# One decoder block on one core: the planner's table of instruction times booked at the distance to the next instruction

## The chip, the core and the metric

The kernel runs on one core of a Trainium2 chip, in 32-bit floats throughout. The metric is device time in microseconds, from one launch. TensorE (PE) multiplies and transposes, VectorE (DVE), ScalarE (ACT) and GpSimd (POOL) work elementwise, SyncE (SP) issues most of the DMAs. Each engine works through a program of its own in order and waits on semaphores.

## What is computed

The reference is a decoder block over 8 rows of 256 tokens with width 256: two Mamba layers, a cross attention, and a mixture of 8 experts with the two best for each token, each followed by a residual and a layer norm. Cut to what matters:

```
for layer in range(2):                                   # Mamba, on x
    u, z = split(x @ in_w.T);  u = silu(causal_conv4(u))
    dt, B, C = split(u @ xp_w.T);  dt = softplus(dt @ dtw.T + dtb)
    h[t] = h[t-1] * exp(dt[t] * A) + (dt[t] * u[t]) * B[t]      # 512 channels x 64 states
    y[t] = sum_over_states(h[t] * C[t]) + u[t] * D_skip
    x = (y * silu(z)) @ out_w.T
x = norm(x0 + x);  x = norm(x + attention(x, ctx));
x = norm(x + sum_k w_k * (relu(x @ w1[e_k] + b1[e_k]) @ w2[e_k] + b2[e_k]))
```

## The kernel before

**Jobs and scans.** One Mamba layer of one row is a job; there are 16, in the order row 0 layer 0, row 1 layer 0, row 0 layer 1, and so on, so that the last job (15) is layer 1 of row 7. A job has 64 states, and each state is one step of the loop: 1024 steps in all, numbered i. In a step ScalarE makes the decay `dA` (L1152, four instructions), TensorE fills the PSUM tile `psX` (`fill_x`: either two transposes that spread B, L1461, after which VectorE multiplies, L1174; or, in a "turned" step, eight transposes of `xs`, L1474, or matmuls with `diag_b`, L1472, after which it need not), VectorE runs the scan over 4 x 256 elements (L1184), GpSimd multiplies with C (L954), and two steps later TensorE adds the product up by eight transposes into `psY` (L1490, `sum_states`). When a job's last state is summed, VectorE multiplies with the gate (L1199). `psX`, `dA`, `h` and `hC` have two or three buffers.

**Work beside the scans.** All other work is cut into tasks: the projections and the convolution of the next job (`tasks_pre`), the output of the last (`tasks_post`), the attention and routing of a finished row (`tasks_row`), and the experts (`tasks_experts`). The rows are routed in four groups of two. Each group gives 15 tiles of 128 slots (tiles 0 to 59; 45 to 59 belong to rows 6 and 7). A tile is gathered by a DMA, transposed (L1693), multiplied with the expert's first weights (8 tasks `hid`, L1437 with `xgT`, in quarters of 256 KB that arrive as `w_up`), goes through ScalarE (`relu`, L1104), is multiplied with the second weights (8 tasks `out`, L1516, `w_down`), copied (`y_copy`, L1111, into the one buffer `yg`) and stored to `y_slots` (L757). When all tiles of a group are stored, the rows are fetched (L916), blended (L1396), normed (`bn3`, `norm3`) and written out (`stored`, L839).

**What sets the order.** The class `Schedule` walks through the 1024 steps before anything is emitted. It keeps a clock for each engine, books each loop instruction and each task with a constant in ns, and puts into the list `beside[i]` those tasks that by its clocks still fit beside step i. The constants decide nothing at run time; they decide which task stands in which step in every engine's program, SP's list of DMAs included. Where the chains for rows and experts are empty, `keep_busy` fills a quarter of TensorE's free time with transposes that nobody reads (L1715). A step that has VectorE tasks is cut into two half scans with the tasks between (`splits`). What does not fit beside the loop stands behind it, in the list `tail`, ordered by `run_off`; there the weights may also use the `dA` and `h` buffers, so that nine quarters are in flight rather than three. The weights of a tile can be loaded only when the group's list of tiles exists (`list`, read by SP at L697).

## Time and profile before

| | us |
|---|---|
| median of 3 runs | 3357.46 (3356.96 to 3365.76) |
| span of the profiled execution | 3358.1 |
| VectorE busy | 3051.3 |
| TensorE busy | 2753.5 |
| ScalarE busy | 2744.4 |
| GpSimd busy | 2659.8 |

For the profiled execution only its span is given, 0.6 us above the median of the three runs. Busy time is the union of recorded lengths; an instruction's record can overlap the next one's, so the recorded length is more than the distance from one start to the next. A matmul of 32-bit operands shows as two records in the trace, a transpose as one.

### The profile page before, as it was taken

The page shows a single profiled execution, that of the slowest core. Times are in us where ns is not written, and L with a number is a line of the kernel's source. Part 1 is how long each engine was busy: PE and PEld are TensorE (multiplying, and loading weights), DVE is VectorE, ACT ScalarE, POOL GpSimd, SP SyncE. Part 2 cuts the span into 40 slices and gives each one's busy share as a digit, 9 for nine tenths or more (in the row PEclk, how much of TensorE's full clock was granted, in tenths as well). Part 3 has the DMA queues.
Part 4 walks back from the last instruction along what each step waited for, and adds up shares of the span by engine and source line. Part 5 has one row for each costly group of instructions (what it writes and reads, how often), then busy time and mean ns, then how long its engine had stood idle before and what let it go on. Part 6 is the DMA issues. An engine that isn't in the chain of part 4 may idle for free.

```text
span 3358.1 us, 55337 instructions
## 1 busy us (share of the span) xinstructions
PE 2753.5 (82%) x19829; PEld 2428.3 (72%) x19829; DVE 3051.3 (91%) x2211; ACT 2744.4 (82%) x6424; POOL 2659.8 (79%) x1289
## 2 busy tenths in 40 slices
PE   6888888887878877888888888878888777888877
PEld 5777777777767767677776777767777666777666
DVE  6999999999999999999999999999999999999510
ACT  7889898898878897897989888898898869888422
POOL 5989898898989788887888788787887878877311
PEclk8999999999999999999999998999999979999988
DMA  3341111111111113223331333313322122443476
GB/s 100 98 145 58 45 51 55 45 55 45 49 60 45 44 47 114 95 77 110 103 116 64 111 119 117 127 64 129 98 102 93 44 88 83 143 132 122 134 263 214
DMA packets 151750, 319.39 MB, mean 95 GB/s; under 512 B 28570, under 2 KB 44963, under 8 KB 151092
## 3 DMA queue, kind: packets, MB, share of 16 engines
q1 hardware_dynamic: 147522, 305.08, 27.5%
q0 software_dynamic: 3072, 8.39, 0.7%
q8 instruction: 158, 2.59, 0.3%
q10 hardware_dynamic: 882, 2.38, 0.2%
q14 instruction: 116, 0.95, 0.1%
HBM read 285.90 MB, written 29.88 MB: 94 GB/s over the span
## 4 chain that ended last, share of the span: by engine, by line
issue 27%; DVE 26%; POOL 19%; ACT 14%; PE 12%; DMA 2%; SPq 1%; POOLq 0%; DVEq 0%; ACTq 0%
POOL hC L954 17%; DVE h L1184 13%; DVE psX L1174 9%; ACT dA L1152 7%; PE psG L1437 3%; PE psY L1490 3%; ACT xs L1123 3%; PE psX L1516 2%; PE psX L1474 1%; PE psX L1472 1%; PE psX L1437 1%; PE psG L1516 1%; ACT gT L1003 1%; DVE gT L1199 1%; ACT scratch L1000 0%
## 5 line engine op out<-in xcount | busy, mean ns | idle before, releaser
L954 POOL TENSOR_TENSOR hC<-h,cb 128x1024 f32<-128x1024 f32 x1024 | 2406.2, 2371 | 496.2 <-DVE h L1184 487.4
L1184 DVE TENSOR_TENSOR_SCAN h<-dA,psX 128x1024 f32<-128x1024 f32 (+1 forms) x1115 | 2306.0, 2102 | 73.2 <-PE psX L1474 30.1
L1152 ACT ACTIVATE dA<-dt,negA 128x255 f32<-128x255 f32 x4096 | 1717.8, 503 | 107.0 <-DVE h L1184 104.9
L1490 PE MATMUL psY<-ident,hC 128*128 128x128 f32 x8192 | 1113.4, 281 | 54.1 <-DVE gT L1199 38.1
L1490 PEld LDWEIGHTS psY<-ident,hC 128*128 128x128 f32 x8192 | 968.1, 145 | 68.8 <-DVE gT L1199 41.7
L1174 DVE TENSOR_TENSOR psX<-dtu,psX 128x1024 f32<-128x1024 f32 x513 | 619.6, 1208 | 10.3 <-PE psX L1461 10.0
L1474 PE MATMUL psX<-ident,xs 128*128 128x128 f32 x3280 | 458.0, 285 | 146.5 <-ACT xs L1123 75.4
L1123 ACT ACTIVATE xs<-dtuT,bT 128x512 f32<-128x512 f32 x820 | 546.1, 719 | 11.9 <-PE psX L1474 11.4
L1474 PEld LDWEIGHTS psX<-ident,xs 128*128 128x128 f32 x3280 | 381.9, 146 | 218.2 <-ACT xs L1123 136.4
L1461 PE MATMUL psX<-ident,bT 128*128 128x128 f32 x1026 | 214.5, 292 | 181.8 <-DVE h L1184 179.8
L1461 PEld LDWEIGHTS psX<-ident,bT 128*128 128x128 f32 x1026 | 116.2, 139 | 283.3 <-DVE h L1184 263.8
L1472 PE MATMUL psX<-diag_b,dtuT 128*128 128x128 f32 x1616 | 212.8, 287 | 60.4 <-DVE h L1184 32.8
L1472 PEld LDWEIGHTS psX<-diag_b,dtuT 128*128 128x128 f32 x1616 | 196.6, 199 | 80.8 <-issue 41.4
L1437 PE MATMUL psG<-xgT,w_up 128*128 128x128 f32 x1456 | 204.2, 284 | 15.2 <-DMA w_up<-in_w_exp 9.1
L1437 PEld LDWEIGHTS psG<-xgT,w_up 128*128 128x128 f32 x1456 | 188.7, 199 | 25.5 <-DMA w_up<-in_w_exp 10.7
L1516 PE MATMUL psG<-w_down,hid 128*128 128x256 f32 x700 | 188.9, 392 | 7.7 <-ACT hid L1104 5.7
L1104 ACT ACTIVATE hid<-psG,b_tile 128x128 f32<-128x128 f32 x408 | 115.3, 366 | 60.7 <-PE psG L1437 60.5
L1516 PEld LDWEIGHTS psG<-w_down,hid 128*128 128x128 f32 x700 | 124.6, 196 | 27.7 <-ACT hid L1104 9.7
L1396 DVE SCALAR_TENSOR_TENSOR acc<-got,slot_weight,acc 128x256 f32<-128x256 f32 x28 | 14.7, 543 | 137.2 <-DMA got<-y_slots,slot_of 127.7
L916 POOL DMA_INDIRECT got<-y_slots,slot_of x28 | 29.1, 1039 | 127.5 <-DMA y_slots<-yg 117.6
L1437 PE MATMUL psG<-xin,w_in 128*128 128x256 f32 x256 | 70.0, 405 | 9.9 <-DMA conv_w<-in_conv 6.1
L1121 ACT ACTIVATE diag_b<-ident,bT 128x128 f32<-128x128 f32 x202 | 69.4, 394 | 4.0 <-PE psX L1472 4.0
(216 smaller groups left out, 2109.3 us busy)
## 6 DMA issues: line engine op xcount, KB each, us to landing
cb<-c_dram SPq DMA_DIRECT2D x256, 512.0 KB
w_up<-in_w_exp SPq DMA_DIRECT2D x196, 256.0 KB
w_down<-in_w_exp SPq DMA_DIRECT2D x196, 256.0 KB
dA<-in_w_exp SPq DMA_DIRECT2D x44, 256.0 KB, 5.5
h<-in_w_exp SPq DMA_DIRECT2D x44, 256.0 KB, 5.4
x_slots<-got SPq DMA_DIRECT2D x16, 512.0 KB, 5.7
xg<-x_slots SPq DMA_DIRECT2D x60, 128.0 KB
y_slots<-yg SPq DMA_DIRECT2D x60, 128.0 KB
```

The costliest lines, as they stand in the source:

```text
L954: eng.tensor_tensor(hC[i % NHC][:, :, :], h[i % NH][:, :, :], cw.to_broadcast([P, KI, L]), ALU.mult).then_inc(times_c, 1)
L1104: made = eng.activation(hid[part][:, i, :], bank[k][:, i * P:(i + 1) * P], ACT.Relu, bias=b1_tile[n % 2][:, c:c + 1])
L1123: made = eng.activation(xs[:, tc, :], dtuT[n % 2][:, tc, :], ACT.Identity, scale=bT[n % 2][:, tc, s:s + 1])
L1152: made = eng.activation(dA[j % NA][:, c, 1:L], dt[n % 2][:, c, 1:L], ACT.Exp, scale=negA[:, JOBS[n][0], c, s:s + 1])
L1174: eng.tensor_tensor(x[:, :, :], dtu[n % 2][:, :, :], x[:, KI - 1:KI, :].to_broadcast([P, KI, L]), ALU.mult).then_inc(times_b, 1)
L1184: made = eng.tensor_tensor_scan(h[i % NH][:, part, :].rearrange("p c t -> p (c t)"), dA[i % NA][:, part, :].rearrange("p c t -> p (c t)"), ...
L1437: made = eng.matmul(dst, lhs, rhs, start=begin and i == 0, stop=end and i == len(terms) - 1)
L1461: made = eng.transpose(psX[i % 2][:, KI - 1, tc * P:(tc + 1) * P], bT[n % 2][:, tc, s:s + 1].to_broadcast([P, P]), ident[:, :])
L1472: made = eng.matmul(to, dtuT[i // S % 2][:, tc, c * P:(c + 1) * P], diag_b[:, tc, :], start=True, stop=True)
L1474: made = eng.transpose(to, xs[:, tc, c * P:(c + 1) * P], ident[:, :])
L1490: made = eng.matmul(psY[:, tc, c * P:(c + 1) * P], hC[i % NHC][:, c, tc * P:(tc + 1) * P], ident[:, :], start=s == 0 and c == 0, stop=s == ...
L1516: made = eng.matmul(bank[k][:, 0:D], hid[half][:, i, :], w_down[slot][:, i % 2, :], start=half == i == 0, stop=half == 1 and i == 3, skip_ ...
```

## The change

The constants are replaced by smaller ones: `MM` (one `hid` or `out` task, half of most others) 520 to 450 ns, `TURN` 130 to 112, `EVICT` 620 to 500, `HALF_EVICT` 470 to 360, a `relu` 4 x 340 to 4 x 260, `SUM` 1060 to 900, `SPREAD` 280 to 250, `OUTER` 1060 to 920, a fill by `diag_b` 2 x 1060 to 1830, `SCALE` 1340 to 1230, the decay 1700 to 1600, the product with C 2380 to 2330, `SCAN` 2220 to 2200. Two are raised: `PRODUCT` 1210 to 1240, and `SPLIT`, the price of cutting a scan in two, 60 to 190. No function that emits instructions is touched.

```diff
-MM, TURN, EVICT, HALF_EVICT = 520, 130, 620, 470
+MM, TURN, EVICT, HALF_EVICT = 450, 112, 500, 360
...
-SUM, SPREAD, OUTER, SCALE, PRODUCT, SCAN, SPLIT = 1060, 280, 1060, 1340, 1210, 2220, 60
+SUM, SPREAD, OUTER, MULTIPLY, SCALE, DECAY, TIMES_C, PRODUCT, SCAN, SPLIT = 900, 250, 920, 1830, 1230, 1600, 2330, 1240, 2200, 190
...
-                at["ACT"] = decay_end[i] = max(at["ACT"], scan_end.get(i - NA, never)) + 1700
+                at["ACT"] = decay_end[i] = max(at["ACT"], scan_end.get(i - NA, never)) + DECAY
```

What moves is the order. Counted in the two orders: before, 43 of the 60 tiles have begun their matmuls beside the loop and 17 stand behind it; now 45 and 15. Per job of 64 steps, `hid` tasks go in jobs 6 to 15 from 16, 27, 41, 33, 43, 32, 40, 8, 40, 64 to 64, 56, 0, 25, 69, 26, 0, 25, 69, 26, and `out` tasks likewise. The transposes of `keep_busy` go from 363 to 1336, steps with a cut scan from 91 to 96.

In the listings below a matmul stands once for each call, whatever its records, and a number behind a name is its buffer.

**TensorE where the loop ends.** `psY<-ident,hC` is the sum of a step, `xgT` and `w_down` are expert tiles, `psX0<-ident,gT` is the first transpose of row 7's output behind the last gate. Before:

```order
L1437 MATMUL psG1<-xgT0,w_up0 128x128 x4
L1490 MATMUL psY<-ident,hC2 128x128 x8
L1490 MATMUL psY<-ident,hC0 128x128 x8
L1516 MATMUL psG0<-w_down0,hid0 128x256 x2
L1516 MATMUL psG0<-w_down1,hid0 128x256 x2
L1516 MATMUL psG0<-w_down2,hid1 128x256 x2
L1516 MATMUL psG0<-w_down0,hid1 128x256 x2
L1693 MATMUL psG1<-ident,xg1 128x128 x2
L1596 MATMUL psX0<-ident,gT 128x128 x8
L1437 MATMUL psX0<-w_out,scratch 128x256 x8
```

Now:

```order
L1490 MATMUL psY<-ident,hC0 128x128 x8
L1490 MATMUL psY<-ident,hC1 128x128 x8
L1490 MATMUL psY<-ident,hC2 128x128 x8
L1490 MATMUL psY<-ident,hC0 128x128 x8
L1596 MATMUL psG0<-ident,gT 128x128 x4
L1596 MATMUL psX0<-ident,gT 128x128 x4
L1437 MATMUL psX0<-w_out,scratch 128x256 x8
L1504 MATMUL psG0<-ident,x1 128x128 x4
```

The tile matmuls that stood around the last sums and ahead of row 7's transposes are gone; they stand some fifty steps earlier.

**SP's list behind the last scan.** `y<-acc` (L839) is the store of a finished row, which waits for VectorE's norm; `dA`, `h`, `w_up`, `w_down` `<-in_w_exp` are quarters of weights; ISA rows work out their addresses. Before, for row 4, among the loads of tiles 45 and 46:

```order
L790 DMA h2<-in_w_exp 128x512
L790 ISA
L790 DMA w_down1<-in_w_exp 128x512
L839 DMA y<-acc 128x512
L790 ISA
L790 DMA w_down2<-in_w_exp 128x512
L790 ISA
L790 DMA w_down0<-in_w_exp 128x512
```

Now both stores of rows 4 and 5 stand ahead of the reading of the last group's list (`tile_at3`), and with it ahead of all its loads:

```order
L839 DMA y<-acc 128x512
L836 DMA acc<-kept 128x512
L814 DMA xrow<-in_x 128x512
L839 DMA y<-acc 128x512
L697 TENSOR_LOAD tile_at3
L698 ISA
L776 DMA w_up0<-in_w_exp 128x512
```

The stores that wait for rows 4 and 5 no longer stand between weight loads.

**TensorE beside job 10.** The rows around the sums of steps 674 to 676; `xs` and `bT` are fills of `psX`, `diag,u0` the skip term, `u1` and `dtu1` the next job's. Before:

```order
L1490 MATMUL psY<-ident,hC1 128x128 x8
L1461 MATMUL psX1<-ident,bT0 128x128 x2
L1497 MATMUL psY<-diag,u0 128x128
L1490 MATMUL psY<-ident,hC2 128x128 x8
L1474 MATMUL psX0<-ident,xs 128x128 x8
L1497 MATMUL psY<-diag,u0 128x128
L1490 MATMUL psY<-ident,hC0 128x128 x8
L1437 MATMUL psG0<-u1,w_x 80x256 x2
L1461 MATMUL psX1<-ident,bT0 128x128 x2
L1497 MATMUL psY<-diag,u0 128x128
```

Now:

```order
L1490 MATMUL psY<-ident,hC1 128x128 x8
L1461 MATMUL psX1<-ident,bT0 128x128 x2
L1497 MATMUL psY<-diag,u0 128x128
L1490 MATMUL psY<-ident,hC2 128x128 x8
L1588 MATMUL psG0<-ident,dtu1 128x128 x4
L1437 MATMUL psG1<-xgT1,w_up0 128x128 x4
L1437 MATMUL psG1<-xgT1,w_up1 128x128 x4
L1474 MATMUL psX0<-ident,xs 128x128 x8
L1497 MATMUL psY<-diag,u0 128x128
L1490 MATMUL psY<-ident,hC0 128x128 x8
```

A dense stretch now has up to four calls of a tile and a piece of the next job between one sum and the fill that the scan waits for.

## Rows read from the trace of the kernel before

**Rows 1.** Windows: stretch, length, busy us of PE, PEld, DVE, ACT, POOL, clock, DMA, GB/s.
```profile
35.00:3138.00 3103.00, 2574.85 (x18781) 2274.38 (x18781) 3009.74 (x2090) 2665.10 (x6196) 2628.53 (x1235) 0.96 0.26 86
3138.00:3187.00 49.00, 36.38 (x202) 29.33 (x202) 14.35 (x58) 11.88 (x36) 3.90 (x4) 0.97 0.35 115
...
3197.00:3246.00 49.00, 27.38 (x150) 23.68 (x151) 8.21 (x22) 8.34 (x29) 9.57 (x10) 0.76 0.73 240
3246.00:3333.00 87.00, 87.00 (x600) 81.25 (x598) 0.00 (x0) 36.27 (x119) 0.00 (x0) 1.00 0.89 295
3333.00:3358.00 25.00, 0.11 (x1) 0.00 (x0) 8.01 (x22) 0.39 (x1) 9.69 (x10) 0.57 0.21 68
```

**Rows 2.** Timeline, VectorE in the loop: start, length, instruction.
```profile
3108.93 4.46 DVE L1184 TENSOR_TENSOR_SCAN h<-dA,psX 128x1024 f32<-128x1024 f32 x2
3113.32 1.21 DVE L1174 TENSOR_TENSOR psX<-dtu,psX 128x1024 f32<-128x1024 f32 x1
...
3120.18 1.22 DVE L1184 TENSOR_TENSOR_SCAN h<-dA,psX 128x512 f32<-128x512 f32 x1
3121.58 0.69 DVE L1220 TENSOR_TENSOR x<-psG,x 128x512 f32<-128x512 f32 x1 [0.18 <-DMA x_slots<-x,slot_of]
...
3125.62 1.21 DVE L1174 TENSOR_TENSOR psX<-dtu,psX 128x1024 f32<-128x1024 f32 x1
```

**Rows 3.** Waits of VectorE, 60 to 3139 us: total, times, longest.
```profile
DVE h L1184 <- PE psX L1474: 30.1, 21, 3.1
DVE h L1184 <- PE psX L1472: 10.5, 8, 3.8
DVE psX L1174 <- PE psX L1461: 10.0, 10, 2.5
```

**Rows 4.** Timeline at the seam of jobs 11 and 12.
```profile
2351.15 1.97 PE L1490 MATMUL psY<-ident,hC 128*128 128x128 f32 x8 [2.93 <-DVE gT L1199]
...
2352.91 3.62 PE L1437 MATMUL psG<-xgT,w_up 128*128 128x128 f32 x16
...
2357.68 2.29 DVE L1184 TENSOR_TENSOR_SCAN h<-dA,psX 128x1024 f32<-128x1024 f32 x1 [3.13 <-PE psX L1474]
```

**Rows 5.** Windows of jobs 10 and 15.
```profile
1937.00:2138.00 201.00, 170.62 (x1202) 150.92 (x1201) 194.91 (x139) 174.96 (x412) 175.29 (x89) 0.94 0.39 124
2938.00:3138.00 200.00, 175.70 (x1311) 158.44 (x1309) 195.75 (x164) 163.01 (x399) 155.25 (x70) 0.98 0.41 133
```

**Rows 6.** Timeline, TensorE: first matmuls of two tiles in a row.
```profile
3253.45 1.95 PE L1437 MATMUL psG<-xgT,dA 128*128 128x128 f32 x16
...
3260.70 1.50 PE L1437 MATMUL psX<-xgT,w_up 128*128 128x128 f32 x12
```

**Rows 7.** Timeline: the pause behind the last scan.
```profile
3214.18 1.05 POOL L916 DMA_INDIRECT got<-y_slots,slot_of  x1 [22.41 <-DMA y_slots<-yg]
...
3227.65 0.35 SPq L839 DMA_DIRECT2D y<-acc  x1
...
3236.64 1.92 DVE L1396 SCALAR_TENSOR_TENSOR acc<-got,slot_weight,acc 128x256 f32<-128x256 f32 x4 [9.02 <-DMA acc<-kept]
...
3239.09 0.38 ACT L1111 ACTIVATE yg<-psX 128x256 f32<-128x256 f32 x1 [19.55 <-DMA y_slots<-yg]
...
3240.56 3.78 PE L1516 MATMUL psX<-h,hid 128*128 128x256 f32 x8 [15.42 <-ACT hid L1104]
```

**Rows 8.** Timeline: last gate, and row 7's first transposes.
```profile
3141.91 1.29 DVE L1199 TENSOR_TENSOR gT<-psY,sz 128x512 f32<-128x512 f32 x2 [3.69 <-PE psY L1490]
...
3146.58 1.04 PE L1596 MATMUL psX<-ident,gT 128*128 128x128 f32 x8
```

**Rows 9.** Timeline: TensorE's waits for weights in tile 45.
```profile
3200.18 2.22 PE L1437 MATMUL psX<-xgT,w_up 128*128 128x128 f32 x16 [1.21 <-DMA w_up<-in_w_exp]
...
3206.93 1.13 PE L1516 MATMUL psX<-w_down,hid 128*128 128x256 f32 x4 [1.72 <-DMA w_down<-in_w_exp]
```

**Rows 10.** Windows: a stretch before the first scan.
```profile
30.00:34.00 4.00, 0.32 (x2) 0.35 (x3) 3.16 (x5) 3.15 (x7) 0.00 (x0) 0.50 0.29 115
```

8 lines of the change are left out of this document (4 added, 4 removed).

## The prediction

> **What bounds the kernel now.** I read the windows first, by stage [rows 1]. The reader is to see two stages. From 35 to 3138 us runs the loop: VectorE is busy for 3009.7 of 3103 us, every other engine clearly less, TensorE 2574.9. Behind the last scan come 220 us in which VectorE hardly works: row 7's own chain, then the last tiles, then the last fetches and norms (25 us, from 3333 on).
>
> In the loop the timeline of VectorE shows the pace [rows 2]: two scans take 4.39 us from start to start (3108.93 to 3113.32), 2.19 each, though a record is longer. So the loop ends when VectorE has done its list, plus what it waits. The list of waits [rows 3] puts the largest down to TensorE's fills of `psX`: 30.1, 10.5 and 10.0 us, 50.6 in 39 times, with up to 3.8 us at once. Where they come from is seen at a seam between jobs [rows 4]: TensorE waited 2.93 us for the gate, then its eight transposes took 1.97 us where the same eight take 1.04 at another place [rows 8], and sixteen tile records took 3.62 us where they take 1.95 [rows 6]; the scan waited 3.13 us for the fill behind them. That is the engine at 1.2 GHz for some microseconds after it had stood still, not too long a list.
>
> Behind the loop I took the timeline. In the steady stretch a tile starts every 7.25 us (3253.45, 3260.70) [rows 6], with TensorE busy for all of 87 us [rows 1]: twelve tiles, 48 to 59. The three before them, 45 to 47, took from 3197 to 3246, 49 us, with TensorE busy for 27.4 of them [rows 1]. The cause stands in [rows 7]. Row 4's fetches wait until the tiles of rows 4 and 5 are stored (3214.18). SP stands at the store of the finished row (3227.65), with weight loads and the next tile's store in its queue behind it; row 5's fetch and blend follow (3236.64). A tile of rows 6 and 7 may be stored in `y_slots` only when both rows are fetched, so `yg` comes free after 19.55 us (3239.09), the `relu` behind it in ScalarE's order waits too, and TensorE has stood for 15.42 us (3240.56).
>
> **The change part by part.** No instruction is added or made faster but for fillers; the order moves. I go through what the moved order meets.
>
> *The pause.* In the new order all tiles of rows 4 and 5 and both fetches stand beside the loop, and both stores stand in SP's list ahead of the reading of the last list of tiles. Nothing of the last group's tiles then waits for them. Tiles 45 to 47 at the pace of the others take 3 x 7.25 = 21.8 us in place of 49.3: **-27.5**. This is what I am surest of.
>
> *Row 7's first transposes.* The gate ends at 3141.91 + 1.29 = 3143.2, the transposes that wait for it alone start at 3146.58 [rows 8], behind tile 42's `out` calls. Those calls are gone from there: **-3.4**.
>
> *Weights at the start.* Tile 45 waited for its weights 1.21 and 1.72 us [rows 9]. These loads cannot start before row 7's list, now as before, so these waits stay within the three tiles: **+3**. The bounds: 0 if the shorter chain leaves them time; on the other side the DMAs as the limit. From 3197 to 3333 they moved 240 x 49 + 295 x 87 = 37.4 MB [rows 1]. At 0.89 busy they gave 295 GB/s, so about 331 at 1.0 (an estimate from that row), and 37.4 MB take 113 us, 4 more than 15 x 7.25 = 109. At 295 GB/s they would take 127, 18 more. I take 3, since row 1's share of 0.89 leaves room. The Trainium skill (DMA: Bandwidth & Descriptors, Specifications) gives about 358 GB/s of HBM for a core; at that the bytes would take 104 us and TensorE would set the pace throughout. No run here shows that rate.
>
> *TensorE's clock in row 7's chain.* Before, tiles 42 to 44 filled TensorE's pauses in that chain: busy 36.4 of 49 us, clock 0.97 [rows 1]. About 16 us of this are tile work (two tiles of 7.25 and parts), so about 20 are the chain's own. Without the tiles the engine has pauses as in the stretch before the first scan, where it was busy for 0.32 of 4 us and granted 0.50 [rows 10]. At half clock a record takes about twice its time [rows 4]. If all of the 20 us fell to it, the chain would be 20 longer, if none, 0. I take a third, **+7**: most of the 20 us are long pieces of some 2 us each that follow close on each other, unlike the stretch of [rows 10]. The Trainium skill (TensorE: Matmul & The Clock Gate, What's actually happening) has it that the array runs at 1.2 GHz when it was idle and at 2.4 when it was busy; [rows 4] agree, 1.97 against 1.04 us. By that rule alone the whole chain, sparse as it is, could be cold: +20 in this term, and the sum 13 higher. This rule speaks against the change in the loop too, since the new constants are the distances at 2.4 GHz.
>
> *VectorE's list in the loop.* From 3197 to 3246 VectorE was busy for 8.21 us [rows 1], with the blends, moments and norms of rows 4 and 5; a blend is 1.92 [rows 7], so moments and norm are about 2.2. Two blends and one set of moments and norm come from behind the last scan to beside it: about 6.0. Five more scans are cut. A cut costs 5.44 (3120.18 to 3125.62) less two scans 4.39, less 0.69 for the work between and 0.18 of waiting [rows 2]: 0.18 each, 0.9. Together 6.9, **+7**.
>
> *VectorE's waits.* Here is the term that can decide. At the distances of [rows 2, 6, 8], TensorE's list beside job 10's scans adds up to 155 us before and 174 now, beside 184 for VectorE: 0.95 of it. Jobs 6, 7 and 14 are like it (0.92, 0.91, 0.95), jobs 8, 12 and 15 go down to about 0.7. ScalarE's list in jobs 10 and 14 comes to 181 of 184. Before, no stretch of eight steps had more TensorE work than VectorE work; now 112 of about 1000 such stretches have. The nearest full job of before is 15: TensorE busy 175.7 of 200 us, clock 0.98 [rows 5]. VectorE was idle there for 200.0 - 195.8 = 4.2 us, and in job 10, with TensorE at 170.6 of 201 and 0.94, for 6.1. So a fuller TensorE has not made VectorE wait, as its clock stays up. From below: behind each of the 15 gates TensorE still has to wait, so one wait like that of [rows 4] stays there; at half its 3.13 us that is some 24 (an estimate), and at most the other 26 of the 50.6 go. From above: every one of the 112 full stretches adds a wait of the mean size, 50.6 / 39 = 1.3 us, to less than a third of them, since they overlap: +45. I take **0**, by job 15's row. The fillers (1336 for 363) take 1.04 / 8 = 0.13 us each [rows 8], but only a quarter of the time that is free in a step, so I count 0; if the three quarters left are not there, they belong to the upper bound.
>
> The sum: -27.5 - 3.4 + 3 + 7 + 7 + 0 = -13.9. Against the profiled span 3358.1, that is 3344.2; the span lies 0.6 above the median of the runs, so 3343.6, say **3344**.
>
> **The rivals.**
> *The loop gives the gain back* (0.17). Waits of VectorE grow by 4 to 24 us, or the DMAs are the limit behind the loop (+4 to +18). For it: 0.95 of VectorE's time for TensorE and 0.98 for ScalarE leave no room for a cold spell such as [rows 4] shows; against it: job 15. Each alone gives 3348 to 3367, so about 3356: no change.
> *Row 7's chain is cold throughout* (0.10). All 20 us of its TensorE work take twice as long, 13 more than in the sum: 3357, no change. For it: the sparse stretch of [rows 10] was granted 0.50; against it: that stretch had 0.32 us of work in 4, the chain has 20 in 49. It is what the Trainium skill's page (TensorE: Matmul & The Clock Gate) has for an engine that idles.
> *The full stretches slow the loop* (0.23). One mechanism: in jobs 6, 7, 10 and 14 TensorE and ScalarE are booked to the brim, each cold spell or late weight load makes the fill late, and nothing later makes up for it, so VectorE loses it one for one. At 1.3 us a wait it decides once it takes more than 24 us (the 13.9 of the sum and 10 of no change), that is from 19 further waits on, about five in each full job; with 20 to 35 of them the time is 3370 to 3390. Against it: VectorE waited no more in job 15 than in emptier jobs.
> *The order behind the loop does not matter* (inside the first rival): if the three tiles ran no faster without the pause, only -3.4 + 7 + 7 would be left, 3368. The busy 87 us [rows 1] speak against it.
> *More than forecast* (inside the forecast): a fuller TensorE stays at 2.4 GHz, the waits outside the seams vanish (-26) and row 7's chain stays warm (-7): 3311.
>
> **How the numbers follow.** A measurement of this kernel can tell about 0.3%, 10 us, from no change: 3347.4 to 3367.5. The forecast, with tail gain and small waits, holds 0.50, all of it faster; its own range is 3322 to 3347. No change has 0.17 + 0.10 = 0.27, slower 0.23. The range of 8 in 10 leaves one in ten below, where the loop's waits go too, and one in ten above: 3322 to 3374.
>
> **What would show it right or wrong.** Right: no wait of ScalarE for `yg` and none of `got` for `y_slots` beyond the last; fifteen tiles at 7.25 us in a row; the last scan near 3145 us, the end some 200 us behind it. The clock from the last scan to row 7's list tells the term of 7: below 0.8 it was too small. Wrong: the last scan later than about 3165, with VectorE's waits for `psX` or `dA` well over 60 us in jobs 6, 7, 10 and 14; or tiles at more than 7.5 us with TensorE waiting for `w_up` and `w_down`.

## The result and the profile after

The changed kernel took **3415.39 us** (median of 4 runs, 3407.83 to 3418.54), beside 3359.89 for the kernel before in the same session (4 runs). The ratio is 1.0159, with a 95% interval of 1.0145 to 1.0172: about 55 us slower, where 3344 had been forecast. The profiled execution had a span of 3406.1 us and a granted clock of 0.943, before 3358.1.

First the windows by stage, which answer to [rows 1]: the loop, row 7's chain, the wait for the last tiles' inputs, the tiles, the end. The columns are as there.

```profile
33.00:3198.00 3165.00, 2683.80 (x19889) 2425.61 (x19887) 3031.64 (x2111) 2679.83 (x6222) 2639.99 (x1244) 0.95 0.26 87
3198.00:3256.00 58.00, 33.74 (x102) 23.75 (x102) 16.69 (x67) 6.27 (x15) 4.99 (x5) 0.62 0.01 5
3256.00:3266.00 10.00, 1.72 (x6) 1.02 (x6) 0.69 (x1) 0.38 (x1) 3.47 (x4) 0.50 0.45 144
3266.00:3381.00 115.00, 111.72 (x747) 103.76 (x745) 0.00 (x0) 44.93 (x148) 0.00 (x0) 0.97 0.89 307
3381.00:3406.00 25.00, 0.03 (x1) 0.00 (x0) 8.01 (x22) 0.38 (x1) 9.69 (x10) 0.59 0.21 69
```

The reader is to see two things. Behind the loop the pause is gone: where TensorE was busy for 27.4 of 49 us and then for all of 87 [rows 1], it is now busy for 111.7 of 115. But the loop is 3165 us long and was 3103. TensorE is busy for 109 us more in it, for the most part with fillers, VectorE for only 22.

From marks in the trace (start of the first scan, end of the last, end of row 7's list of tiles) the 48 us between the two spans divide thus. "Idle" is the sum of all pauses of VectorE between its instructions, that is the loop's length less VectorE's busy time in it; where an expectation below names an idle time, it is counted some 4 to 5 us higher (96.9 us before, 137.9 after).

| part | before | after | difference |
|---|---|---|---|
| up to the first scan | 34.8 | 33.6 | -1.2 |
| loop, VectorE idle | 93.3 | 133.3 | +40.0 |
| loop, VectorE's own list | 3010.1 | 3031.3 | +21.2 |
| last scan to row 7's list | 49.2 | 57.7 | +8.5 |
| the rest | 170.6 | 150.2 | -20.4 |

The waits of VectorE from 35 to 3198 us, total, times and longest, answer to [rows 3] (there from 60 us on; here 4.3 us of the second row, in three times, lie ahead of 60):

```profile
DVE h L1184 <- PE psX L1474: 44.2, 45, 4.7
DVE psX L1174 <- PE psX L1461: 33.2, 35, 3.1
DVE h L1184 <- ACT dA L1152: 12.3, 15, 2.4
```

The scans' wait for `xs` fills grew from 30.1 to 44.2 us in 45 times for 21, and the multiplies' wait for the spread fills from 10.0 to 33.2 in 35 for 10: not a few long stops, but many more of about 1 us or less. Most of it lies where the prediction had said that it would show: in jobs 6, 7, 10 and 14 VectorE's idle time rose from 19 to 47 us, in jobs 9 and 13 from 10 to 20, and in jobs 0 to 5, which hold no tile, it stayed at 42. What stood behind the longest of all is seen in the timeline of TensorE and VectorE near the end of job 7:

```profile
1502.75 0.50 PE L1437 MATMUL psG<-xgT,w_up 128*128 128x128 f32 x3
1508.41 1.23 PE L1437 MATMUL psG<-xgT,w_up 128*128 128x128 f32 x4 [5.16 <-DMA w_up<-in_w_exp]
1509.43 1.91 PE L1474 MATMUL psX<-ident,xs 128*128 128x128 f32 x8
...
1511.38 2.29 DVE L1184 TENSOR_TENSOR_SCAN h<-dA,psX 128x1024 f32<-128x1024 f32 x1 [4.66 <-PE psX L1474]
```

A `hid` piece stands in TensorE's order ahead of the fill that the next scan needs. Its weights are late, TensorE stands for 5.16 us, the fill behind it is cold (1.91 for eight, 1.04 where warm; the granted clock from 1508.4 to 1511.4 is 0.50), and VectorE loses 4.66 us. TensorE's list of waits shows how often such stops came:

```profile
PE psG L1437 <- DMA w_up<-in_w_exp: 28.9, 21, 5.2
```

Before, the same row from 60 to 3139 us reads as follows; one of its times, of 0.9 us, lies behind the last scan, so in the loop they were 8.2 us in 7 times.

```profile
PE psG L1437 <- DMA w_up<-in_w_exp: 9.1, 8, 2.3
```

VectorE's own list grew by 21 us and not by 7. One reason is in the timeline: the division of the attention weights (two instructions of 128x256), in the gap between two half scans. Before, in job 7, GpSimd's instruction ends at 1496.69 (1494.31 + 2.38) and no other follows for 1.68 us:

```profile
1494.31 2.38 POOL L954 TENSOR_TENSOR hC<-h,cb 128x1024 f32<-128x1024 f32 x1
...
1496.55 0.62 DVE L1301 TENSOR_SCALAR prob<-prob,small 128x256 f32<-128x256 f32 x2
```

After, in the same job, GpSimd has its next instruction at once:

```profile
1424.44 1.23 POOL L880 TENSOR_TENSOR scratch<-scratch,gT 128x506 f32<-128x506 f32 x1
...
1424.38 1.44 DVE L1301 TENSOR_SCALAR prob<-prob,small 128x256 f32<-128x256 f32 x2
```

The same two instructions take 1.44 us for 0.62. The second ends at 1425.82, 0.15 behind GpSimd's (1424.44 + 1.23 = 1425.67). Six such pairs in the loop have a second of about 1.17 us; before, one had, of 1.35. Counted over all of VectorE's instructions in the loop that are neither scan nor multiply, the records grew by 12.5 us (148.7 to 161.2). The 15 instructions more account for about 6. The rest is length above the shortest record of the same instruction: 15.7 us in 24 instructions before, 22.4 in 36 after, and every one of them overlaps an instruction of GpSimd. No run took GpSimd's work away, so that GpSimd is the cause is read from these records and not tested.

### The profile page after: what moved, and what is told of

Read it like the earlier page. It is cut to its first block, busy times and chain, and to the rows that moved or that the text cites. A ratio compares the mean times of both kernels' runs of the same rounds, so it can differ in the third digit from the quotient of the medians.

```text
span 3406.1 us, 57278 instructions
## 1 busy us (share of the span) xinstructions
PE 2847.0 (84%) x20802; PEld 2565.1 (75%) x20802; DVE 3066.1 (90%) x2216; ACT 2751.3 (81%) x6424; POOL 2662.4 (78%) x1289
## 3 DMA queue, kind: packets, MB, share of 16 engines
q10 hardware_dynamic: 882, 2.38, 0.2%
## 4 chain that ended last, share of the span: by engine, by line
PE 31%; issue 18%; ACT 17%; DVE 16%; POOL 13%; DMA 4%; SPq 1%; POOLq 0%; DVEq 0%; ACTq 0%
POOL hC L954 11%; DVE h L1184 8%; PE psY L1490 8%; PE psG L1437 8%; ACT dA L1152 8%; DVE psX L1174 5%; PE psX L1474 4%; PE psG L1516 4%; ACT xs L1123 3%; PE psX L1437 2%; DMA w_up<-in_w_exp 2%; PE psX L1472 2%; DMA w_down<-in_w_exp 1%; PE psX L1461 1%; ACT hid L1104 1%
## 5 line engine op out<-in xcount | busy, mean ns | idle before, releaser
L1184 DVE TENSOR_TENSOR_SCAN h<-dA,psX 128x1024 f32<-128x1024 f32 (+1 forms) x1120 | 2311.3, 2094 | 87.0 <-PE psX L1474 44.2
L1490 PEld LDWEIGHTS psY<-ident,hC 128*128 128x128 f32 x8192 | 982.8, 147 | 46.7 <-DVE gT L1199 36.1
L1174 DVE TENSOR_TENSOR psX<-dtu,psX 128x1024 f32<-128x1024 f32 x513 | 620.2, 1209 | 34.8 <-PE psX L1461 33.2
L1474 PE MATMUL psX<-ident,xs 128*128 128x128 f32 x3280 | 471.0, 291 | 151.2 <-DVE h L1184 81.6
L1474 PEld LDWEIGHTS psX<-ident,xs 128*128 128x128 f32 x3280 | 398.5, 150 | 208.8 <-ACT xs L1123 101.1
L1472 PE MATMUL psX<-diag_b,dtuT 128*128 128x128 f32 x1616 | 206.7, 282 | 41.2 <-ACT diag_b L1121 22.4
L1437 PE MATMUL psG<-xgT,w_up 128*128 128x128 f32 x1440 | 193.9, 280 | 34.0 <-DMA w_up<-in_w_exp 28.9
L1516 PE MATMUL psG<-w_down,hid 128*128 128x256 f32 x804 | 204.8, 384 | 11.5 <-DMA w_down<-in_w_exp 7.1
L1437 PEld LDWEIGHTS psG<-xgT,w_up 128*128 128x128 f32 x1440 | 177.7, 194 | 47.0 <-DMA w_up<-in_w_exp 33.2
L1715 PE MATMUL psG<-ident 128*128 128x128 f32 x1336 | 193.1, 274 | 0.0
L1516 PEld LDWEIGHTS psG<-w_down,hid 128*128 128x128 f32 x804 | 140.6, 190 | 33.8 <-DMA w_down<-in_w_exp 13.9
L1715 PEld LDWEIGHTS psG<-ident 128*128 128x128 f32 x1336 | 156.0, 142 | 4.1 <-issue 2.8
L1104 ACT ACTIVATE hid<-psG,b_tile 128x128 f32<-128x128 f32 x360 | 101.7, 368 | 36.7 <-PE psG L1437 36.6
```

The lines of the kernel that those rows point to most:

```text
L1174: eng.tensor_tensor(x[:, :, :], dtu[n % 2][:, :, :], x[:, KI - 1:KI, :].to_broadcast([P, KI, L]), ALU.mult).then_inc(times_b, 1)
L1184: made = eng.tensor_tensor_scan(h[i % NH][:, part, :].rearrange("p c t -> p (c t)"), dA[i % NA][:, part, :].rearrange("p c t -> p (c t)"), ...
L1437: made = eng.matmul(dst, lhs, rhs, start=begin and i == 0, stop=end and i == len(terms) - 1)
L1472: made = eng.matmul(to, dtuT[i // S % 2][:, tc, c * P:(c + 1) * P], diag_b[:, tc, :], start=True, stop=True)
L1474: made = eng.transpose(to, xs[:, tc, c * P:(c + 1) * P], ident[:, :])
L1490: made = eng.matmul(psY[:, tc, c * P:(c + 1) * P], hC[i % NHC][:, c, tc * P:(tc + 1) * P], ident[:, :], start=s == 0 and c == 0, stop=s == ...
```

## The experiments

Eighteen kernels ran, beside the kernel before on the same chip each time. The table holds, for all of them: median, ratio with interval, and from the one profiled execution the loop (start of first to end of last scan), VectorE's idle time in it, and the pauses over 0.1 us divided by TensorE's clock. "Cold" are those where the granted clock was at its half level (1.2 GHz) for more than 0.4 us of the 4 us before the pause's end, "warm" the others. This rule of counting is my choice, and it decides the split: asked for more than 1.6 us of the 4, before has 40.7 cold and 24.0 warm, after 48.0 and 56.0, e5 43.9 and 45.1, e22 30.6 and 33.7. Only a difference that both rules show is used below. "Low" is the time in the loop at that level, "vector" the records of VectorE in the loop that are neither scan nor multiply. All in us.

| run | median | ratio (95%) | loop | idle | cold | warm | low | vector |
|---|---|---|---|---|---|---|---|---|
| before | 3359.89 | 1 | 3103.4 | 93.3 | 43.1 | 21.6 | 260 | 148.7 |
| after | 3415.39 | 1.0159 (1.0145-1.0172) | 3164.6 | 133.3 | 54.8 | 49.2 | 304 | 161.2 |
| e1_mm_turn_only | 3340.81 | 0.9946 (0.9929-0.9963) | 3089.7 | 84.3 | 33.2 | 22.4 | 246 | 144.2 |
| e2_loop_constants_only | 3351.51 | 0.9972 (0.9956-0.9988) | 3106.6 | 97.9 | 45.8 | 23.6 | 280 | 145.8 |
| e3_no_fillers | 3435.78 | 1.0231 (1.0200-1.0262) | 3190.2 | 157.5 | 81.6 | 47.0 | 434 | 160.6 |
| e5_four_weight_slots | 3393.17 | 1.0091 (1.0065-1.0117) | 3146.7 | 118.0 | 58.0 | 31.0 | 317 | 161.4 |
| e6_warm_chain | 3413.61 | 1.0153 (1.0130-1.0175) | 3176.9 | 145.7 | 66.0 | 50.4 | 317 | 160.9 |
| e8_tensor_constants_only | 3359.48 | 0.9985 (0.9972-0.9997) | 3113.9 | 102.5 | 36.9 | 36.6 | 280 | 145.1 |
| e4_room_400_less | 3402.40 | 1.0123 (1.0106-1.0139) | 3154.1 | 132.8 | 60.6 | 43.5 | 318 | 152.0 |
| e9_slots_and_warm | 3342.55 | 0.9942 (0.9926-0.9959) | 3100.1 | 93.8 | 45.1 | 19.8 | 281 | 144.2 |
| e18_tensor_lighter_tiles | 3413.40 | 1.0167 (1.0145-1.0189) | 3166.3 | 135.5 | 72.6 | 33.5 | 372 | 161.3 |
| e19_scalar_lighter_tiles | 3411.29 | 1.0152 (1.0135-1.0169) | 3170.3 | 138.0 | 59.7 | 48.9 | 303 | 162.8 |
| e11_scalar_task_constants_old | 3365.22 | 1.0004 (0.9990-1.0019) | 3116.5 | 106.3 | 38.9 | 38.9 | 260 | 143.6 |
| e15_room_and_four_slots | 3384.27 | 1.0080 (1.0060-1.0101) | 3140.1 | 121.6 | 57.5 | 35.4 | 331 | 152.1 |
| e20_tensor_half_tiles | 3412.22 | 1.0140 (1.0123-1.0156) | 3173.1 | 143.8 | 88.6 | 26.3 | 417 | 161.1 |
| e21_slots_and_half_tiles | 3405.40 | 1.0128 (1.0111-1.0145) | 3157.1 | 128.5 | 74.3 | 25.1 | 399 | 162.1 |
| e22_old_scalar_tasks_four_slots | 3352.24 | 0.9972 (0.9961-0.9982) | 3100.4 | 92.5 | 34.2 | 30.1 | 264 | 144.3 |
| e23_slots_half_tiles_light_scalar | 3395.36 | 1.0103 (1.0086-1.0119) | 3150.7 | 121.9 | 65.3 | 27.3 | 379 | 161.7 |
| e24_hop_220 | 3395.88 | 1.0083 (1.0067-1.0100) | 3152.1 | 132.9 | 55.8 | 48.0 | 319 | 150.1 |
| e25_hop_220_four_slots | 3388.81 | 1.0067 (1.0050-1.0084) | 3144.2 | 126.7 | 63.3 | 34.4 | 328 | 150.7 |

One profiled execution is a rough gauge of a loop: the orders of after and of e6 are the same up to the last scan, and their loops took 3164.6 and 3176.9 us. So differences of some 12 us between single profiles prove nothing; the medians decide. Between sessions the kernel before itself moved from 3359.9 to 3364.7, so runs of different sessions are best compared by their ratios.

**Which constants.** Two parts of the change alone. e2 is written against the changed kernel and leaves of the change only the loop's own constants.

```diff
# e1_mm_turn_only, on the kernel before
-MM, TURN, EVICT, HALF_EVICT = 520, 130, 620, 470
+MM, TURN, EVICT, HALF_EVICT = 450, 112, 620, 470
# e2_loop_constants_only, on the changed kernel
-MM, TURN, EVICT, HALF_EVICT = 450, 112, 500, 360
+MM, TURN, EVICT, HALF_EVICT = 520, 130, 620, 470
-            out.append(task("relu", t, half, "ACT", 4 * 260, ...
+            out.append(task("relu", t, half, "ACT", 4 * 340, ...
```

> The kernel before with only MM 520 to 450 and TURN 130 to 112; everything else keeps the old constants. Its TensorE list beside the loop is hardly fuller than before (0.72 to 0.86 of VectorE's list per job, 3 full stretches of eight steps for 112 in the change), but all tiles of rows 4 and 5 stand beside the loop, so the pause behind the last scan is gone. Theory A (the loop lost its time because TensorE's list is booked full): the loop ends within 10 us of the 3138 us of before, and the kernel is 5 to 20 us faster than before. Rival B (the smaller task constants of themselves break the order, however full): the loop ends later than 3155 us and the kernel is not faster.

> The changed kernel with the constants of the tasks (MM, TURN, EVICT, HALF_EVICT, relu) back at the old ones; the loop's own constants stay the new ones. TensorE's list is up to 0.89 of VectorE's, 7 full stretches of eight steps. Theory A (fullness): loop end between, near 3150 us, and a total within 10 us of before. Rival B (task constants alone at fault): as A. Rival C (the loop's own constants at fault): loop end near the changed kernel's 3198 us and a total near its 3415.

Both are faster than the kernel before, 20 and 10 us by the medians of their session (3361.11 before). So either part alone is of use; the loss needs what is in neither, or the two together. Two more runs narrowed it:

```diff
# e8_tensor_constants_only, on the changed kernel
-MM, TURN, EVICT, HALF_EVICT = 450, 112, 500, 360
+MM, TURN, EVICT, HALF_EVICT = 450, 112, 620, 470
-SUM, SPREAD, OUTER, MULTIPLY, SCALE, DECAY, TIMES_C, PRODUCT, SCAN, SPLIT = 900, 250, 920, 1830, 1230, 1600, 2330, 1240, 2200, 190
+SUM, SPREAD, OUTER, MULTIPLY, SCALE, DECAY, TIMES_C, PRODUCT, SCAN, SPLIT = 900, 250, 920, 1830, 1340, 1700, 2380, 1210, 2220, 60
-            out.append(task("relu", t, half, "ACT", 4 * 260, ...
+            out.append(task("relu", t, half, "ACT", 4 * 340, ...
# e11_scalar_task_constants_old, on the changed kernel: the first and the third of these edits alone
```

> The kernel before with all of TensorE's constants of the change (450, 112, sum 900, spread 250, outer 920, multiply 1830) and the old ones for ScalarE, GpSimd, VectorE and the split. Its lists have 61 stretches of eight steps in which TensorE's work is more than VectorE's (0 before, 112 in the changed kernel, 3 with the constants 450 and 112 alone). Theory of the full stretches: the loop's end moves with their number, 61 of 112, so the last scan ends 20 to 45 us later than with 450 and 112 alone (3126), at 3146 to 3170, with VectorE's waits above 80 us. Rival (ScalarE's and GpSimd's constants make the loop slow, because the relu stand too close): last scan at 3126 to 3140, waits as with 450 and 112 alone (56 to 65 us).

> The changed kernel with the old constants for ScalarE's tasks alone (620, 470 and 340 for 500, 360 and 260). Stretches of eight steps with more TensorE work than VectorE work, fillers not counted: 0 in the kernel before, 44 with TensorE's constants alone, 60 here, 89 in the changed kernel; with more ScalarE work than VectorE work: 121 before, 171, 180 here, 208 in the changed kernel. Theory of the full stretches, whichever engine: between the run with TensorE's constants alone (last scan 3148.8) and the changed kernel, 3160 to 3178, the run at 3372 to 3388. Rival (ScalarE's task constants alone make the difference): 3140 to 3152, the run at 3350 to 3362.

e8 ended at the time of before. Its last scan, at 3148.8, lies in the range of the theory of full stretches (3146 to 3170); VectorE's waits for `psX` were 60 us, as its rival had them. e11 came out at 3365, between that theory's range (3372 to 3388) and its rival's (3350 to 3362), its last scan at 3151.8: nearer the rival. Against the kernel before, all new constants but those of ScalarE's tasks cost nothing, though they give back the 20 us that 450 and 112 alone had gained (3341). 500, 360 and 260 on top of them cost 50 us (3415 for 3365): that these three numbers, on top of the others, make nearly all of the loss is shown. No run has them alone. What they do to the order is the rest of the question.

**Late weights.** Four buffers for quarters of weights beside the loop and, with those of `dA` and `h`, ten behind it. The expectations call the ten "tile slots"; the kernel keeps weights in them.

```diff
# e5_four_weight_slots, on the changed kernel; e22 has the same edit on e11
-NW = 3
-NT = 9
+NW = 4
+NT = 10
```

> The changed kernel with four buffers for quarters of expert weights instead of three (ten instead of nine behind the loop); the order of everything else is the same. Theory E (the denser runs of tiles outrun three weight buffers; TensorE then waits for a quarter with the fill behind it): TensorE's waits for w_up in the loop fall from 28.9 us to under 10, VectorE's waits for psX fall by 15 to 25 us, and the kernel is 15 to 30 us faster than the changed one. Theory A (full lists alone): the waits for w_up fall, but the kernel gains under 8 us.

> The changed kernel with the old constants for ScalarE's tasks (that run: 3365, last scan 3151.8, TensorE's waits for w_up in the loop 23.0 us) and with four weight slots and ten tile slots. Theory (late weights count by what stands before VectorE's waits: 15.5 us there): the run at 3345 to 3353, last scan near 3136. Rival (they only count in the full jobs of the changed order): 3360 to 3368.

With four slots TensorE no longer waited for weights in the loop at all, and the run was 22 us faster than the changed kernel (3393 for 3415), as its theory had it; in e22 it was 13 faster than e11 (11 by the ratios), again as expected. VectorE's waits of e5, over the whole run:

```profile
DVE h L1184 <- PE psX L1474: 31.0, 33, 2.4
DVE psX L1174 <- PE psX L1461: 28.9, 25, 3.8
```

The first is back at the 30.1 of [rows 3], the second, with its 4.0 us ahead of 60, is not. This cause is shown by an experiment: some 22 of the 55 us. e22 has the idle time of the kernel before (92.5 for 93.3). e5 and e22 differ in ScalarE's task constants alone, and in 41 us.

**Fillers and room.**

```diff
# e3_no_fillers, on the changed kernel
-            if many > 0:
+            if False:
# e4_room_400_less, on the changed kernel; e15 has it with four slots
-WINDOW, PE_OVER, FIRST, LONG, HOP, NEAR = 24, 0, 1500, 3300, 100, 60
+WINDOW, PE_OVER, FIRST, LONG, HOP, NEAR = 24, -400, 1500, 3300, 100, 60
```

> The changed kernel without any filler transpose (L1715); no result uses them. Theory D (the 1336 fillers delay the fills and the scans): jobs 0 to 5 and 8 get shorter and the kernel is 10 to 20 us faster than the changed one. Theory A: fillers stand in free time, so no gain, within 5 us of the changed kernel, or some us slower, since TensorE stands at 1.2 GHz more often in those jobs.

> The changed kernel, with 400 ns less room for TensorE in each step of the loop (PE_OVER -400 for 0); all constants stay. The full stretches of eight steps fall from 112 to 83. Theory of the full stretches, by their number: of the 60 us that the loop lost about a quarter comes back, last scan at 3175 to 3190. If what counts is how tight each single step is filled, more comes back, down to 3150. Rival (weights that come late, or VectorE's own longer work): last scan within 5 us of 3198.

> The changed kernel with both: 400 ns less room for TensorE in each step, and four weight slots and ten tile slots for three and nine. Each alone brought 13 and 22 us. If they mend separate causes (late weights; full steps) they add up, and the run is at 3375 to 3383, ratio to the kernel before 1.005; if both mend the same waits, it is at 3388 to 3396.

Without the fillers the kernel is 20 us slower still, more than either side had expected, and the low clock holds for 434 us of the loop and not 304: the fillers are no cost, they are what keeps TensorE's clock up. Less room brought 13 us, though the idle time did not move (132.8 for 133.3) and the last scan, at 3190.3, stands at the edge of the theory's range (3175 to 3190); what went down is VectorE's other work (152.0 for 161.2). Fewer vector tasks stand beside the loop (467 instructions for 478, 93 cut steps for 96), and the lengths beside GpSimd fell from 22.4 to 17.3 us. With four slots the two gains add up for the most part: 31 us (27 by the ratios), of 13 + 22, a result between the two that had been expected.

**Is an engine's list too full?** This was the rival of the prediction, and my theory for most of the loss. The next five runs keep the changed order and take work away from an engine; what they leave out is missing from the experts' sums.

```diff
# e18_tensor_lighter_tiles: for the tiles 0 to 44
-                made = eng.matmul(bank[k][:, 0:D], hid[half][:, i, :], w_down[slot][:, i % 2, :],
+                made = eng.matmul(bank[k][:, 0:to], hid[half][:, i, :], w_down[slot][:, i % 2, 0:to],
# to is 64 for seven of eight; likewise the second product of each hid piece, 32 of 128 columns
# e19_scalar_lighter_tiles
-                        for i in range(4):
+                        for i in range(1 if 2 <= n < TILE0[-2] else 4):
# e20_tensor_half_tiles: as e18, but three out products and every second hid product left out
# e21: e20 with four slots;  e23: e21 with the edit of e19
```

> The changed kernel in its own order, with every task in its place, but with less to do for TensorE in the tiles 0 to 44: of a tile's 8 out products 7 have 64 columns for 256, and of its 16 hid products 8 have 32 for 128. It leaves out this part of the experts' sums. At 0.45 us a pair of columns blocks this takes some 3.7 of a tile's 7.25 us from TensorE, so that its list in the full jobs 6, 7, 10 and 14 falls from 0.92 of VectorE's to about 0.8. ScalarE, the transfers and VectorE's list stay. Theory (TensorE is booked to the brim, and its lateness makes VectorE wait): most of the growth of the waits goes, VectorE's idle time from 138 us to 90 to 105, the last scan from 3198 to 3150 to 3168. Rival 1 (the order itself, or ScalarE's full list): idle time above 125, last scan above 3185. Rival 2 (late weights): like rival 1, since the transfers stay as they are.

> The changed kernel in its own order, with less to do for ScalarE in the tiles 2 to 44: each relu task evicts one of its four 128x128 blocks and leaves out three, so 2.2 us less of ScalarE's work for each tile, some 18 of the 181 us in the full jobs. It leaves out this part of the experts' sums. TensorE, the transfers and VectorE's list stay. Theory (TensorE's full list is what makes VectorE wait): last scan within 10 us of 3198, idle time of VectorE above 125. Rival (ScalarE's full list delays relu, xs and the decays, and with them TensorE): idle time below 110, last scan at 3150 to 3175.

> The changed kernel in its own order, with more than half of TensorE's work in the tiles 0 to 44 left out: the second of the two products of each hid piece, three of the eight out products, and of four others the last 192 of 256 columns. The experts' sums lack these parts. That is about 4.0 of a tile's 7.25 us, so some 33 of the 177 us in the jobs 10 and 14, where 8.3 tiles stand. Transfers, ScalarE and VectorE stay. Theory (TensorE booked to the brim): waits for psX fall from 86 to below 65 us, last scan at 3155 to 3175. Rival (only the late weights and the places of the pieces count): last scan within 8 us of 3198, idle time of VectorE above 125 us.

> As the one before, with four weight slots and ten tile slots for three and nine; the run with these slots alone had its last scan at 3181.7, VectorE idle for 122.6 us, and took 3393. Theory (brim): the remaining 26 us of idle time over the kernel before (96.9) go for the most part, last scan at 3152 to 3165, the run at 3363 to 3376. Rival: within 6 us of 3181.7 and 3393.

> The changed kernel with four weight slots and ten tile slots, more than half of TensorE's work in the tiles 0 to 44 left out, as above, and three of four evicting relu instructions of the tiles 2 to 44 left out as well. What is left of the tiles is their order, their transfers and VectorE's blends. Theory (a full list of either engine): last scan below 3158, idle time of VectorE near the 97 us of the kernel before. Rival (the order itself): last scan above 3172, idle time above 115 us.

e18 took less from TensorE than I had counted. Its timeline, beside the same place of the changed kernel:

```profile
2008.41 0.55 PE L1517 MATMUL psG<-w_down,hid 128*128 128x64 f32 x4
2008.80 1.04 PE L1474 MATMUL psX<-ident,xs 128*128 128x128 f32 x8
```

```profile
2010.83 0.59 PE L1516 MATMUL psG<-w_down,hid 128*128 128x256 f32 x2
2011.26 0.38 PE L1461 MATMUL psX<-ident,bT 128*128 128x128 f32 x2
```

From start to start a record of 64 columns takes 0.39 / 4 = 0.10 us, one of 256 takes 0.43 / 2 = 0.215, not a quarter of it. The likely floor is the weights' load: from 2008 to 2010 us of e18 the load side of the engine was busy for 1.95 of 2.00 us. The Trainium skill (TensorE: Matmul & The Clock Gate, LDWEIGHTS) has such a load take 128 / 1.2 = 107 ns for 128 columns of weights; the distance here, 98 ns, is near that and a little less.

e20 took away what it should. These are the windows of jobs 6, 7, 10 and 14, of the changed kernel and then of e20:

```profile
1156.00:1351.00 195.00, 173.14 (x1301) 160.31 (x1300) 185.66 (x104) 176.73 (x425) 165.34 (x78) 0.96 0.45 148
1351.00:1567.00 216.00, 192.61 (x1366) 173.50 (x1365) 198.52 (x163) 182.98 (x439) 165.69 (x81) 0.95 0.36 120
1980.00:2175.00 195.00, 176.94 (x1330) 162.43 (x1329) 184.63 (x102) 179.33 (x433) 161.17 (x75) 0.98 0.45 146
2796.00:2991.00 195.00, 177.96 (x1332) 163.95 (x1331) 184.93 (x101) 179.61 (x433) 161.30 (x75) 0.97 0.44 144
```

```profile
1156.00:1351.00 195.00, 152.21 (x1135) 137.66 (x1135) 186.92 (x104) 176.71 (x428) 164.81 (x78) 0.96 0.47 148
1351.00:1567.00 216.00, 172.48 (x1217) 155.11 (x1215) 200.45 (x166) 184.81 (x443) 168.16 (x81) 0.92 0.38 123
1980.00:2175.00 195.00, 157.48 (x1167) 141.74 (x1166) 185.42 (x102) 179.77 (x435) 162.57 (x76) 0.94 0.46 147
2796.00:2991.00 195.00, 156.58 (x1133) 141.76 (x1131) 183.92 (x101) 179.29 (x433) 160.92 (x75) 0.92 0.45 144
```

TensorE is busy for some 20 us less in each of them (33 had been counted, at the warm pace), and VectorE is busy for as long as before within 2. The kernel was no faster, 3412 for 3415, and with four slots it was 12 us slower than with the whole tiles (3405 for 3393). The table shows why: the warm waits fell, from 49.2 to 26.3, and from 31.0 to 25.1 with four slots; the cold ones rose from 54.8 to 88.6, and from 58.0 to 74.3, and the low clock held for 417 and 399 us of the loop. By the stricter rule the warm ones fell from 56.0 to 38.8 and from 45.1 to 31.5, and the cold ones rose from 48.0 to 76.1 and from 43.9 to 67.8. Here the engine with less to do was at 1.2 GHz for longer, and VectorE waited more behind it. In e20 a second thing stood in the way: the tiles were done sooner and TensorE waited longer for `w_up`, 47.4 us for 28.9. In e21 it waited for no weights at all, so the pair e5 and e21 is the cleaner one. The full list did cost something, 6 us of warm waits in that pair by the one rule and 14 by the other. More cannot be said of it, since the same edit adds a cost through the clock; but more room by itself gives nothing back. For ScalarE it is plainer: in e19 it had 9 to 14 us less to do in the four full jobs, and nothing moved (3411 for 3415, idle 138.0 for 133.3). With all three edits (e23) the run stayed at e5's time. Where less work was to give time back, the forecast failed in all five runs.

**Results booked too early?** A distance says how long an engine is taken, not when the result can be read. The planner adds `HOP`, 100 ns, for a reader on another engine; 220 gives back what the change took off an eviction.

```diff
# e24_hop_220, on the changed kernel; e25 has it with four slots
-WINDOW, PE_OVER, FIRST, LONG, HOP, NEAR = 24, 0, 1500, 3300, 100, 60
+WINDOW, PE_OVER, FIRST, LONG, HOP, NEAR = 24, 0, 1500, 3300, 220, 60
```

> The changed kernel with all its constants, and 220 ns for 100 between the end of a task and its reader on another engine (HOP). 120 ns is what the change took off an eviction (620 to 500, 470 to 360). The list stays as uneven as in the changed kernel: eight tiles beside the scans of jobs 10 and 14 each, none or one beside 8 and 12. Theory (results are booked too early, readers stand in order before they can run): of the 41 us of further idle time the part that is not from weights goes, idle time 138 to 110 to 120, last scan at 3165 to 3178, the run at 3380 to 3392. Rival (the uneven order and the vector work cut in between the scans are what costs): idle time above 130, last scan within 8 us of 3198.

> As the one before, with four weight slots and ten tile slots for three and nine. Theory: both causes of idle time gone, idle time 97 to 105 us, last scan at 3145 to 3160, the run at 3358 to 3372; what is left over the run with ScalarE's old task constants and four slots (3352) is VectorE's own longer work, some 10 us beside GpSimd. Rival: as four slots alone, last scan 3181, the run at 3390 to 3396.

e24 was 20 us faster than the changed kernel (26 by the ratios), e25 only 4 faster than e5 (8 by the ratios), and both came out above the theory's ranges. The idle time, of which the theory spoke, did not fall (132.9 for 133.3; 126.7 for 118.0). So the theory is not borne out: what fell is VectorE's other work, 161.2 to 150.1, as in e4, and the cut scans (93 steps for 96). That part of the gain is seen in the traces; where the rest comes from is not shown.

**Row 7's chain kept warm.** Transposes into an idle bank between the chain's pieces.

```diff
# e6_warm_chain, on the changed kernel; e9 has it with four slots on e1
         self.run_off(self.tail, ("G", "U0", "U1"), ("M", "B0", "B1"))
+        self.keep_warm()
...
+        for p in self.tail:
+            out.append(p)
+            if p in behind:
+                out.append(("keep", 9000 + len(out), behind[p]))
```

> The changed kernel, and between the pieces of row 7's chain behind the last scan 4 to 36 transposes more, into a bank that nothing reads, so that TensorE has something to do while it waits for VectorE and ScalarE. The output stays as it is. Theory (the chain is longer because TensorE falls to 1.2 GHz once the tiles 42 to 44 no longer fill its pauses): from the last scan to row 7's list 57.6 us comes down to 49 to 51, the granted clock of that stretch from 0.62 to above 0.85, the run is 6 to 9 us faster than the changed kernel, about 3407; the loop ends as before at about 3198. Rival (the chain is longer because its waits for VectorE and ScalarE are its own): clock up, length within 2 us of 57.6, and the run as slow as the changed kernel or slower, since the added transposes stand in front of the pieces.

> The kernel before with 450 and 112 for a tile's matmuls and transposes as its only constants of the change, with four weight slots and ten tile slots for three and nine, and the transposes of the warm chain behind the last scan. 450 and 112 alone gave 3341. Theory: the late weights are gone (7.8 us of TensorE's waits in the loop, worth 3 to 6 us of VectorE's), the chain is 3 to 6 us shorter where its tiles leave it cold: 3325 to 3337. Rival: four slots help only where the lists are full; then 3338 to 3343.

The chain of e6, windows:

```profile
3213.00:3265.00 52.00, 39.40 (x210) 32.12 (x210) 16.84 (x67) 6.27 (x15) 4.82 (x5) 0.80 0.02 6
```

From the last scan to the list it took 51.6 us for 57.7, and in e9 52.3 for the 58.9 of e1. The other changed orders, without added transposes, took 54.8 to 58.9. So some 6 of the 8.5 us by which the chain had grown are the clock; the theory had 49 to 51 us at a clock above 0.85, and it was 0.80. The median fell by less, 1.8 us, within its interval. On e1 slots and warm chain together brought nothing that can be told (3342.6 for 3340.8, in two sessions), as that run's rival had it and not its theory (3325 to 3337).

## Why the prediction was wrong, step by step

*The pause* (-27.5) *and the weights at the start* (+3): together -24.5 forecast, -20.4 measured. The mechanism was right: no wait for `yg`, no store between the weight loads, and tiles in a row at 7.24 us. (The sum has 49.3 us for the three tiles where [rows 1] have 49, which is 0.3 us.) The rest of the difference lies at the start: the first tile waits 7.80 us for its input and the pieces behind it are cold (24 records in 4.83 us, 16 take 1.95 in [rows 6]).

```profile
3264.14 0.66 PE L1693 MATMUL psG<-ident,xg 128*128 128x128 f32 x2 [7.80 <-DMA xg<-x_slots]
3265.27 4.83 PE L1437 MATMUL psX<-xgT,w_up 128*128 128x128 f32 x24 [0.47 <-ACT xgT L1092]
...
3306.67 0.38 PE L1693 MATMUL psX<-ident,xg 128*128 128x128 f32 x2
...
3313.91 0.38 PE L1693 MATMUL psX<-ident,xg 128*128 128x128 f32 x2
```

*Row 7's transposes and the clock in its chain* (-3.4 + 7 = +3.6): +8.5 measured. The transposes did come sooner, 6.0 us behind the last scan (3204.21) and not 8.4 (3146.58 - 3138.2, [rows 8]). The clock's term was too small, as the prediction's own mark (below 0.8) says: 0.62, where it had been 0.97 [rows 1]. So 2.4 of the 3.4 came, since the sum ahead of the gate was itself cold (1.97 us for eight), and 10.9 are left for the clock's term, of which e6 gave 6.1 back.

```profile
3206.93 5.81 PE L1437 MATMUL psX<-w_out,scratch 128*128 128x256 f32 x16 [0.78 <-ACT scratch L1055]
```

This one piece, 16 records of 256 columns, is 5.81 us long, where eight such records in [rows 7] show 3.78 cold and a warm run of eight takes 1.89 (3299.64 of the changed kernel): some 2 us more than twice 1.89. "A third" of a cold chain was a number without a row, and the long pieces did not keep the clock up.

*VectorE's list* (+7): +21.2 measured. This is the second step that failed, by its size. The moved vector work and five more cuts are there as foreseen, 478 instructions for 463 and 192 half scans for 182. What I had no term for: vector instructions beside GpSimd's (some 7 us of the 12.5), and the scans, whose mean from start to start went from 2.197 to 2.206 us, or 8 us over 928. The runs with more idle time have the longer distances (2.208 at 157 us idle, 2.198 at 84), so this goes with the waits: a scan that nothing follows at once shows its whole record (2.29 us above) and not the 2.19 at which the next one starts.

*VectorE's waits* (0, bounds -26 to +45): +40.0 measured, near the upper bound. This is the step that decided. That "a fuller TensorE has not made VectorE wait", by job 15's row, was an inference from a mean share [rows 5] to an order of a different shape. What the runs show in its place is what a tight row of tiles asks for: eight tiles of weights in 190 us through three slots. The pauses over 0.1 us grew by 39.3 us: with four slots 15.0 of it goes (in the loop's idle time 15.3, in the median 22). That is the part whose cause an experiment shows. Of the 24.3 that stay, 9.4 are warm and 14.9 cold by the first rule of counting, 21.1 and 3.2 by the stricter one, so how much of them is the clock and how much TensorE's full list stays open.

*The rivals.* "The full stretches slow the loop" had the right sign and nearly the size of the waits; it gave 3370 to 3390, and the rest of the way is the other terms: 3344 + 40.0 for the waits, 14.2 more for the list, 4.9 for the chain and 4.1 for the tiles is 3407, less 1.2 up to the first scan, beside a span of 3406.1. It had 20 to 35 further waits of 1.3 us; the three rows of waits for `psX` went from 39 times to 92, at 0.9 us. Its mechanism is right in one half, late weight loads that nothing makes up for, and not borne out in the other: it had ScalarE and TensorE "booked to the brim", and taking work away from either brought nothing. Of the rivals behind the loop, the cold chain was half right: the clock fell to 0.62 and cost 10.9 us, where that rival had 20. The DMAs did not set the pace (tiles at 7.24 us), and the order behind the loop did matter.

*What stays open.* The last 41 us between e5 and e22, which differ in ScalarE's task constants alone. 17 us are VectorE's records beside the scans (161.4 for 144.3): 6 for the 15 instructions more, 11 for lengths beside GpSimd (22.4 for 11.1). Another 25 are pauses (89.0 for 64.3). The changed order bunches the tiles (eight beside jobs 10 and 14, none beside 8 and 12) and so leaves TensorE long sparse stretches. That fits the runs without fillers and with half tiles, but between e5 and e22 the traces bear it out in part only: of the 25.5 us of idle time 8 lie in jobs 0 to 5, which hold no tile in either, and 10 in jobs 9 and 13; e22 has no tile beside job 12 either; and in jobs 8, 9, 12 and 13 together the low clock holds for 161 us in e5 and for 150 in e22. No run spread the tiles and kept the rest.

## What to carry to other kernels

A planner's constants are also its margins: shortening them all at once to measured distances moved work into places where the loads were late and where VectorE's instructions met GpSimd's, while one pair of them alone (450 and 112) made this kernel 0.54% faster. Judge an order by the stops it makes, and where an engine's clock falls when it has less to do, as TensorE's did here, don't count on time back from giving it less. Before a split into two kinds of waits carries an argument, move the line between them and see whether it holds. A mean share of busy time says nothing on whether the next load is in time.
